# Exact attention scores in two halves of TensorE's rows, and new orders for the steps ahead of the loop

## The chip, the core and the metric

The kernel runs on one core of one Trainium2 chip. The metric is the device time of one execution in microseconds (us); smaller is better. TensorE is PE in the profile (its weight loads are PEld), VectorE is DVE, ScalarE is ACT, GpSimd is POOL, and the queue of SyncE that issues most transfers is SPq.

## The reference

64 sequences of 128 tokens and 128 features go through a block with two residual parts. Softmaxes are over keys.

```python
x = x + tanh(g_xattn) * cross_attention(layernorm(x), ctx)         # 16 heads of 8, 120 keys of ctx
x = x + tanh(g_ffn) * block(layernorm(x))
# block(x):
h = rms(x, n1_w); q = rms(heads(h @ wq.T), qn_w); k = rms(heads(h @ wk.T), kn_w); v = heads(h @ wv.T)
ao = softmax(where(causal, q @ k.T * HD**-0.5, -inf)) @ v @ wo.T   # 16 heads of 8, 128 keys
x = x + ao                                                         # features 0:32 of ao set to zero
xf = rms(x, n2_w); gates = top-2 softmax of xf @ gate_w.T          # four experts
x = x + sum_e gates_e * expert_e(xf)                               # features 0:32 of the sum set to zero
```

## The kernel before

The work is cut into 16 groups of G = 4 sequences and into five parts: N (layer norm, queries and keys of the cross attention), A (cross attention), B (queries and keys of the self attention), D (self attention and the first expert matmuls) and M (the rest of the experts). One step works on a different group in each part: M on the oldest, N on the newest. Every engine's program runs through the same list of works of a step. Four steps with lists of their own fill the pipeline (`first_group`, `second_group`, `third_group`, `fourth_group`; the text calls them the first, second, third and fourth step), twelve steps of the hardware loop share one list (`SCHEDULE`), and four more empty it (`last_queries`, `last_self_keys`, `last_self_values`, `last_experts`). A list says in which order each engine meets the works and which of the eight PSUM banks each of them takes (rings `w` of four banks, `s2` or `f` of the banks s2a and s2b, `pv`, `t`). An engine issues its instructions strictly in this order, and semaphores count how often a bank was filled and drained.

Each attention score is computed twice. The *estimate* (`s1`, L1299, bf16) gives the maximum over keys: for a sequence b and a set c of four heads, K = 32 rows of TensorE at a time; the four sets take the four row groups and four banks, and DVE reduces each bank (L1085, into `mpad`, or `mhalf` in the steps ahead of the loop). The maxima are transposed (works `mT`, or `mH` and `mL` for the first and the last two sequences apart), copied by ACT and stored by DMA as one row of the query tile `qd`. The *exact* score (`s2`, L1335, fp32r) is a matmul of 512 columns on stacks of split numbers: `kst` holds 24 rows for each of four heads and a row of ones, `qd` the four heads' queries on a block diagonal, zeros elsewhere, and the maxima in row 96, so that the maximum is subtracted on the way. ACT takes the exponential of the bank (L945, 512 columns) into a slot of `probs`; the self attention's slots are masked by POOL; then 16 small matmuls to a sequence (`pv`, L1356) multiply by the values. `exact(part, b, c)` in a list is the two sets c and c + 1 of sequence b, one in bank s2a and one in s2b: the text calls it a pair. There are 16 pairs in a step with A and D, 8 of each.

Around the exact scores the lists put estimates, values, transposes (L1218), and matmuls with all 128 rows in fp32: qk (L1267), down (L1382), the hidden layers (L1394, L1401). On `qd` and `kst` the zeros and ones are written once, before the first step; stacks are loaded by SP from `scratch`, after both operands were stored there.

## Time and profile before

| what | us |
|---|---|
| median of three runs | 1086.48 (1086.42 to 1088.23) |
| the profiled execution, its own time | 1085.92 |
| its span, from the first to the last instruction | 1084.2 |
| PE busy | 1011.1 |
| DVE busy | 790.0 |
| ACT busy | 736.9 |
| POOL busy | 338.4 |

The span holds the first step (0 to 25), the second (to 57), the third (to 98), the fourth (to 161), the twelve passes of the loop, and the four last steps. A busy TensorE is not TensorE at its peak: a matmul is counted from its issue to its last write, and matmuls overlap.

### The profile page before, as it was taken

The numbers are of one execution on the slowest core, as the hardware profiler recorded it, in microseconds if no ns is written. First come the engines' busy times: TensorE is split into PE (matmuls) and PEld (weight loads), VectorE is DVE, ScalarE is ACT, GpSimd is POOL, SyncE is SP. The second block draws the span as 40 slices with busy tenths as digits, with TensorE's granted clock in tenths as the row PEclk, the third lists the DMA queues.
The fourth block names the chain that finished last, engine by engine and source line by source line (L and its number), as shares of the span: only waits on it lengthen the run. The fifth ranks groups of instructions, "written<-read, shape, count | busy, mean of one in ns | idle before, by whom it ended". The sixth has DMA issues, their size and how long they took to land.

```text
span 1084.2 us, 26207 instructions
## 1 busy us (share of the span) xinstructions
PE 1011.1 (93%) x8649; PEld 628.9 (58%) x8649; DVE 790.0 (73%) x2172; ACT 736.9 (68%) x1334; POOL 338.4 (31%) x463
## 2 busy tenths in 40 slices
PE   7666799999999999999999999999999999999898
PEld 5343456666565566655665665566556565555465
DVE  8546787778778777877777777878777877784633
ACT  6464576677776768777676777767676777757353
POOL 5253315151330505133150514214141422404140
PEclk9779799999999999999999999999999999999999
DMA  6305233334322243333224343332233333221200
GB/s 231 121 27 195 86 101 103 127 115 143 110 94 94 90 126 124 133 114 111 93 73 124 130 127 114 123 99 84 97 129 127 114 134 104 84 67 62 68 1 19
DMA packets 77316, 114.26 MB, mean 105 GB/s; under 512 B 7776, under 2 KB 40160, under 8 KB 77152
## 3 DMA queue, kind: packets, MB, share of 16 engines
q1 hardware_dynamic: 76736, 111.51, 31.7%
q10 hardware_dynamic: 544, 2.28, 0.6%
q8 instruction: 22, 0.36, 0.1%
q14 instruction: 14, 0.11, 0.0%
HBM read 58.97 MB, written 53.74 MB: 104 GB/s over the span
## 4 chain that ended last, share of the span: by engine, by line
PE 64%; DVE 16%; ACT 13%; issue 6%; DMA 1%; ACTq 0%; POOL 0%; DVEq 0%
PE ps_pv L1356 9%; PE ps_w L1382 9%; PE ps_s2a L1335 7%; PE ps_s2b L1335 5%; PE ps_s2a L1394 5%; PE ps_s2b L1401 4%; ACT probs L945 4%; PE ps_t L1218 4%; DVE mpadB L1085 3%; PE ps_w L1401 3%; DVE mpadA L1085 3%; PE ps_w L1267 3%; PE ps_t L1369 3%; PE ps_w L1299 2%; PE ps_w L1218 2%
## 5 line engine op out<-in xcount | busy, mean ns | idle before, releaser
L945 ACT ACTIVATE probs<-ps_s2a 120x512 f32<-120x512 f32 (+1 forms) x256 | 153.6, 600 | 73.7 <-PE ps_s2a L1335 65.3
L1085 DVE TENSOR_REDUCE mpadB<-ps_w 128x4 f32<-128x512 f32 x240 | 148.8, 684 | 24.9 <-PE ps_w L1299 24.9
L1085 DVE TENSOR_REDUCE mpadA<-ps_w 128x4 f32<-128x480 f32 x224 | 131.5, 651 | 41.0 <-PE ps_w L1299 41.0
L945 ACT ACTIVATE probs<-ps_s2b 120x512 f32<-120x512 f32 (+1 forms) x256 | 153.5, 600 | 0.0
L812 POOL TENSOR_SCALAR_AFFINE_SELECT probs<-probs 128x1024 f32<-128x1024 f32 x128 | 140.2, 1095 | 0.0
L1382 PE MATMUL ps_w<-W,hid 128*128 128x96 f32 x1008 | 125.3, 278 | 1.8 <-DVE split_k L979 0.9
L1382 PEld LDWEIGHTS ps_w<-W,hid 128*128 128x128 f32 x1008 | 117.5, 192 | 12.0 <-issue 6.4
L776 POOL TENSOR_TENSOR rB<-vrB,neg_half 128x4 f32<-128x4 f32 x16 | 16.1, 1009 | 204.3 <-DVE veB L972 204.3
L1335 PE MATMUL ps_s2a<-qdA,kstA 128*120 128x512 f32 x128 | 68.5, 535 | 10.6 <-ACT probs L945 9.2
L1114 DVE SCALAR_TENSOR_TENSOR ym<-ps_w,gates,ym 128x96 f32<-128x96 f32 x192 | 47.6, 311 | 39.5 <-PE ps_w L1382 39.5
L1335 PE MATMUL ps_s2a<-qdB,kstB 128*128 128x512 f32 x128 | 65.2, 509 | 11.1 <-DMA qdB<-mTlB 4.5
L1394 PE MATMUL ps_s2a<-hid,W 128*128 128x512 f32 x152 | 74.5, 605 | 0.0
L949 ACT ACTIVATE oT<-ps_pv 128x512 f32<-128x512 f32 x64 | 38.3, 598 | 53.0 <-PE ps_pv L1356 53.0
L941 ACT ACTIVATE hid<-ps_s2a 128x512 f32<-128x512 f32 x75 | 45.0, 600 | 42.6 <-PE ps_s2a L1394 31.0
L1356 PE MATMUL ps_pv<-probs,VA 120*18 120x128 f32 x2048 | 69.3, 276 | 0.0
L1356 PE MATMUL ps_pv<-probs,VB 128*18 128x128 f32 x2048 | 69.3, 276 | 0.0
L952 ACT ACTIVATE onT<-ps_t 128x256 f32<-128x256 f32 x64 | 24.6, 385 | 61.1 <-PE ps_t L1218 61.1
L811 POOL TENSOR_TENSOR tick<-one 128x1 f32<-128x1 f32 x128 | 25.0, 196 | 127.4 <-ACT probs L945 123.6
L1356 PEld LDWEIGHTS ps_pv<-probs,VA 120*18 120x18 f32 x2048 | 50.9, 98 | 22.7 <-issue 21.4
L1356 PEld LDWEIGHTS ps_pv<-probs,VB 128*18 128x18 f32 x2048 | 50.9, 98 | 17.7 <-issue 17.1
L1335 PE MATMUL ps_s2b<-qdA,kstA 128*120 128x512 f32 x128 | 59.0, 461 | 0.0
L1369 PEld LDWEIGHTS ps_t<-W,onT 128*128 128x128 f32 x256 | 39.2, 196 | 32.4 <-issue 20.1
(276 smaller groups left out, 2133.8 us busy)
## 6 DMA issues: line engine op xcount, KB each, us to landing
scratch_Aq<-split_q SPq DMA_DIRECT2D x48, 256.0 KB, 2.4
qdA<-scratch_Aq SPq DMA_DIRECT2D x64, 192.0 KB
scratch_Bq<-split_q SPq DMA_DIRECT2D x48, 256.0 KB, 2.4
scratch_Bk<-split_k SPq DMA_DIRECT2D x48, 256.0 KB, 3.0
qdB<-scratch_Bq SPq DMA_DIRECT2D x64, 192.0 KB
kstB<-scratch_Bk SPq DMA_DIRECT2D x64, 192.0 KB
scratch_Ak<-split_k SPq DMA_DIRECT2D x48, 240.0 KB, 2.4
kstA<-scratch_Ak SPq DMA_DIRECT2D x64, 180.0 KB
```

Of the source, the lines that this page charges most:

```text
L812: pool.affine_select(out=tile, in_=tile, compare_op=ALU.is_ge, fill=0.0, base=0, pattern=[[0, 2 * HT], [1, P]], channel_multiplier=-1).the ...
L941: nc.scalar.activation(hid[:, HID_AT[index[0]] + index[1], :], bank[:], ACT.Gelu).then_inc(done, 1)
L945: nc.scalar.activation(probs[0:k, slot_of(part, *index), :], bank[0:k, :], ACT.Exp, scale=SCALE if part == "A" else 1.0).then_inc(done, 1)
L1085: nc.vector.tensor_reduce(pair[:, :, c, b % 2] if halves else mneg[p][:, :, c, b], bank[:, 0:HT * k].rearrange("p (h k) -> p h k", h=HT), ...
L1114: ins = nc.vector.scalar_tensor_tensor(out=ym[:, b, KEEP:P], in0=bank[:, b * UP:(b + 1) * UP], scalar=gates[:, b, e:e + 1], in1=y[:, b, KE ...
L1218: ins = nc.tensor.transpose(psum[st.bank[key]][:, b * P:(b + 1) * P], of(b), identf[:])
L1335: mm(o, kst[p][:, c, b * k:(b + 1) * k], qd[p][:, :, c, b * P:(b + 1) * P], start=True, stop=True).then_inc(done, 1)
L1356: ins = mm(psum[st.bank[last]][32 * j:32 * j + VS, at:at + P], VB[p][0:k, first:first + VS], probs[0:k, slot_of(part, b, c), j * P:(j + 1) ...
L1369: ins = mm(bank[:, s * n:(s + 1) * n], onT[:, s * P:(s + 1) * P], w["Wo"] if part == "A" else w["wo"], start=True, stop=True)
L1382: ins = mm(bank[:, b * UP:(b + 1) * UP], hid[:, HID_AT[h] + k, b * P:(b + 1) * P], w[f"down{index[1]}"][:, k * UP:(k + 1) * UP], start=k = ...
L1394: ins = mm(bank[:], w[name][:, k * HID + c * P:k * HID + (c + 1) * P], hid[:, HID_AT[h] + k, :], start=k == 0, stop=k == chunks[-1])
L1401: mm(bank[:], w[name][:, c * P:(c + 1) * P], xfT[:], start=True, stop=True).then_inc(done, 1)
```

## The change

An exact matmul now takes half of the rows: rows 0 to 48 hold heads 0 and 1 of a set with a row of maxima (row 48), rows 64 to 112 heads 2 and 3 with another (row 112). `qd` needs two column blocks of queries instead of four, and each half is a matmul of 49 rows and 256 columns. A pair (sets c and c + 1) becomes four such matmuls, in the order: lower half of c into bank s2a, upper half of c into s2b, lower half of c + 1 into s2a, upper half of c + 1 into s2b. So bank s2a ends with heads 0 and 1 of both sets, s2b with heads 2 and 3 of both, and the values are read from the new places. Ahead of the first of the four, PE waits for both banks to be drained; each bank's count rises with its last matmul. The number of columns, of exponentials and of DMA bytes stays. Half as many zeros are written ahead.

```diff
-        qd = {p: sb("qd" + p, [P, HT, NT, TOK], F32R) for p in "AB"}
+        qd = {p: sb("qd" + p, [P, HT // 2, NT, TOK], F32R) for p in "AB"}
...
-        M_ROW = HD * SPLIT * HT
+        HALF_ROWS, M_ROW = P // 2, HD * SPLIT * HT // 2
...
+        def rows_of_head(j):
+
+            first = j // 2 * HALF_ROWS + j % 2
+            return slice(first, first + M_ROW, 2)
...
-                        for bk, v in st.drains([], key):
-                            pe.wait_ge(drained[bk], v)
-                        o = bank[0:k, :].rearrange("p (h q) -> p h q", h=HT)
-                        mm(o, kst[p][:, c, b * k:(b + 1) * k], qd[p][:, :, c, b * P:(b + 1) * P],
-                           start=True, stop=True).then_inc(done, 1)
+                        if c % 2:
+                            continue
+                        tiles = [(part, "s2", (b, c + half)) for half in range(2)]
+                        for tile in tiles:
+                            for bk, v in st.drains([], tile):
+                                pe.wait_ge(drained[bk], v)
+                        for cc in range(2):
+                            for half in range(2):
+                                rows = slice(half * HALF_ROWS, half * HALF_ROWS + M_ROW + 1)
+                                o = psum[st.bank[tiles[half]]][0:k, cc * 2 * P:(cc + 1) * 2 * P].rearrange("p (h q) -> p h q", h=2)
+                                ins = mm(o, kst[p][rows, c + cc, b * k:(b + 1) * k], qd[p][rows, :, c + cc, b * P:(b + 1) * P],
+                                         start=True, stop=True)
+                                if cc:
+                                    ins.then_inc(filled[st.bank[tiles[half]]], 1)
...
-            clear_queries("A", 2, 3, setup_act)
...
-                            clear_queries("B", 0, HT // 2, b_cleared)
+                            clear_queries("B", 0, 1, b_cleared)
```

The lists of the second, third and fourth step are new. With them `mL` of A's first group goes by SP's queue instead of ACT's, and POOL makes the causal factor of the keys right after that of the queries, one step earlier. In `last_queries` one work moves by one place, and in `last_self_keys` the last two down matmuls take bank pv, estimate 2 stands between them, and estimate 3 stands ahead of the second half of the first expert. The loop's list is the same.

```diff
-    return (one("N", "xT", 0, "pv") + one("N", "k", 0, "t") + one("N", "q", 0, "pv") + one("A", "mL")
-            + exact("A", 0, 0) + exact("A", 0, 2) + estimate("A", 0) + exact("A", 1, 0) + exact("A", 1, 2) + values("A", 0)
+    return (one("N", "xT", 0, "pv") + one("N", "k", 0, "t") + exact("A", 0, 0) + one("A", "mL") + exact("A", 0, 2) + one("N", "q", 0, "pv")
+            + exact("A", 1, 0) + estimate("A", 0) + exact("A", 1, 2) + values("A", 0)
```

ACT's instructions at the start of the second step, before: the casts of keys and queries (L850, L855), the copy of the maxima (L915) with its transfer, then the exponentials.

```order
L850 ACTIVATE kTbA<-ps_t,vc 128x480
L855 ACTIVATE split_k<-ps_t,vc 128x480
L850 ACTIVATE qTbA<-ps_pv,vc 128x512
L855 ACTIVATE split_q<-ps_pv,vc 128x512
L915 ACTIVATE mTlA<-ps_w 32x128
L924 DMA qdA<-mTlA 1x16x128 x2
L945 ACTIVATE probs<-ps_s2a 120x512
L945 ACTIVATE probs<-ps_s2b 120x512
```

And in the changed kernel:

```order
L860 ACTIVATE kTbA<-ps_t,vc 128x480
L865 ACTIVATE split_k<-ps_t,vc 128x480
L952 ACTIVATE probs<-ps_s2a 120x512
L952 ACTIVATE probs<-ps_s2b 120x512
L922 ACTIVATE mTlA<-ps_w 32x128
L952 ACTIVATE probs<-ps_s2a 120x512
L952 ACTIVATE probs<-ps_s2b 120x512
L860 ACTIVATE qTbA<-ps_pv,vc 128x512
```

Two exponentials move ahead of the queries' casts, and the transfer leaves ACT's queue.

DVE's instructions in the third step, before: the split and the spread keys of the self attention (L979, L987), then the first maxima of its estimates (`mhalfB`), behind the output matmul's sum (L1136).

```order
L1124 RECIPROCAL rden<-ps_t 128x32
L1126 TENSOR_TENSOR on<-ps_t,rden 128x256
L1001 TENSOR_SCALAR xn<-xt,mvA,rsA 128x128 x4
L979 SCALAR_TENSOR_TENSOR split_q<-ps_w,qns,split_q 128x512
L987 TENSOR_SCALAR kdB<-kTbB,pick 128x512 x4
L979 SCALAR_TENSOR_TENSOR split_k<-ps_w,vc,split_k 128x512
L1136 SCALAR_TENSOR_TENSOR x<-ps_t,tg,xb 128x256
L1085 TENSOR_REDUCE mhalfB<-ps_s2a 128x4
L1085 TENSOR_REDUCE mhalfB<-ps_s2b 128x4
```

In the changed kernel:

```order
L986 SCALAR_TENSOR_TENSOR split_q<-ps_w,qns,split_q 128x512
L994 TENSOR_SCALAR kdB<-kTbB,pick 128x512 x4
L986 SCALAR_TENSOR_TENSOR split_k<-ps_w,vc,split_k 128x512
L1008 TENSOR_SCALAR xn<-xt,mvA,rsA 128x128 x4
L1131 RECIPROCAL rden<-ps_t 128x32
L1133 TENSOR_TENSOR on<-ps_t,rden 128x256
L1092 TENSOR_REDUCE mhalfB<-ps_w 128x4 x4
L1143 SCALAR_TENSOR_TENSOR x<-ps_t,tg,xb 128x256
L1092 TENSOR_REDUCE mhalfB<-ps_s2a 128x4
```

The split keys come ahead of the oT work (`rden`, `on`), and the first four maxima ahead of the sum.

PE's instructions from the first exact pair of the fourth step on, before: the transpose of the last maxima (L1316) stands behind the first values (L1356).

```order
L1335 MATMUL ps_s2b<-qdB,kstB 128x512
L1218 MATMUL ps_w<-identf,hb 128x128 x4
L1335 MATMUL ps_s2a<-qdB,kstB 128x512
L1335 MATMUL ps_s2b<-qdB,kstB 128x512
L1267 MATMUL ps_w<-W,hT 128x256 x4
L1335 MATMUL ps_s2a<-qdB,kstB 128x512
L1335 MATMUL ps_s2b<-qdB,kstB 128x512
L1299 MATMUL ps_w<-kdA,qTbA 128x480 x4
L1335 MATMUL ps_s2a<-qdB,kstB 128x512
L1335 MATMUL ps_s2b<-qdB,kstB 128x512
L1356 MATMUL ps_pv<-probs,VB 18x128 x16
L1316 MATMUL ps_t<-identf,mhalfB 32x128
```

In the changed kernel:

```order
L1254 MATMUL ps_w<-W,ctT 120x128 x4
L1279 MATMUL ps_w<-W,hT 128x128 x4
L1323 MATMUL ps_t<-identf,mhalfB 32x128
L1349 MATMUL ps_s2a<-qdB,kstB 128x256
L1349 MATMUL ps_s2b<-qdB,kstB 128x256
L1349 MATMUL ps_s2a<-qdB,kstB 128x256
L1349 MATMUL ps_s2b<-qdB,kstB 128x256
L1225 MATMUL ps_w<-identf,hb 128x128 x4
L1349 MATMUL ps_s2a<-qdB,kstB 128x256
L1349 MATMUL ps_s2b<-qdB,kstB 128x256
L1349 MATMUL ps_s2a<-qdB,kstB 128x256
L1349 MATMUL ps_s2b<-qdB,kstB 128x256
```

The transpose now stands ahead of the step's first pair, and each pair has four matmuls of 256 columns.

## Rows read from the trace of the kernel before

**Rows 1.** The page: busy time of each engine; the chain that ended last.

```profile
PE 1011.1 (93%) x8649; PEld 628.9 (58%) x8649; DVE 790.0 (73%) x2172; ACT 736.9 (68%) x1334; POOL 338.4 (31%) x463
PE 64%; DVE 16%; ACT 13%; issue 6%; DMA 1%; ACTq 0%; POOL 0%; DVEq 0%
```

**Rows 2.** Busy time and clock (PEclk) in four stretches.

```profile
25.00:57.00 32.00, 20.64 (x193) 11.31 (x192) 18.12 (x44) 13.98 (x27) 11.20 (x22) 0.78 0.35 112
57.00:98.00 41.00, 29.36 (x244) 18.56 (x244) 24.74 (x68) 23.47 (x43) 14.06 (x26) 0.84 0.26 87
98.00:161.00 63.00, 51.64 (x453) 31.04 (x453) 45.00 (x114) 38.74 (x74) 19.35 (x25) 0.89 0.33 108
480.00:543.00 63.00, 61.66 (x539) 38.18 (x537) 48.87 (x135) 45.85 (x86) 19.85 (x26) 1.00 0.34 113
```

**Rows 3.** Chain, same place in two passes: start, us, what.

```profile
480.09 0.23 PE ps_s2a L1335
...
542.63 0.23 PE ps_s2a L1335
```

**Rows 4.** Timeline, a pair behind an estimate and ahead of values: start, us.

```profile
489.66 0.50 PE L1335 MATMUL ps_s2a<-qdB,kstB 128*128 128x512 f32 x1
489.77 0.19 PEld L1335 LDWEIGHTS ps_s2b<-qdB,kstB 128*128 128x128 f32 x1
490.00 0.40 PE L1335 MATMUL ps_s2b<-qdB,kstB 128*128 128x512 f32 x1
490.32 0.79 PEld L1356 LDWEIGHTS ps_pv<-probs,VB 128*18 128x18 f32 x32 [0.36 <-issue]
```

**Rows 5.** Timeline, PE, a pair's second matmul ahead of transposes with 128 rows.

```profile
488.20 0.39 PE L1335 MATMUL ps_s2b<-qdB,kstB 128*128 128x512 f32 x1
488.44 0.60 PE L1218 MATMUL ps_t<-identf,oT 128*128 128x128 f32 x4
```

**Rows 6.** Timeline, weight loads of an estimate, one for each row group.

```profile
82.71 0.09 PEld L1295 LDWEIGHTS ps_s2a<-causal_k,causal_q 32*128 32x128 bf16 x1
...
82.72 0.10 PEld L1295 LDWEIGHTS ps_w<-causal_k,causal_q 32*128 32x128 bf16 x2
```

**Rows 7.** Timeline, weight loads of down, all in the same rows.

```profile
475.84 1.86 PEld L1382 LDWEIGHTS ps_w<-W,hid 128*128 128x128 f32 x16
```

**Rows 8.** Timeline, dense stretch: an exponential and weight loads of pairs.

```profile
480.88 0.60 ACT L945 ACTIVATE probs<-ps_s2b 128x512 f32<-128x512 f32 x1
...
481.54 0.19 PEld L1335 LDWEIGHTS ps_s2b<-qdB,kstB 128*128 128x128 f32 x1 [0.30 <-ACT probs L945]
...
482.97 0.19 PEld L1335 LDWEIGHTS ps_s2a<-qdB,kstB 128*128 128x128 f32 x1 [0.21 <-issue]
...
484.64 0.19 PEld L1335 LDWEIGHTS ps_s2b<-qdB,kstB 128*128 128x128 f32 x1 [0.30 <-ACT probs L945]
```

**Rows 9.** Timeline, last self values: first matmuls of two pairs in a row.

```profile
1028.25 0.48 PE L1335 MATMUL ps_s2a<-qdB,kstB 128*128 128x512 f32 x1
...
1029.42 0.49 PE L1335 MATMUL ps_s2a<-qdB,kstB 128*128 128x512 f32 x1 [0.45 <-ACT probs L945]
```

**Rows 10.** Timeline, second step: ACT's key split, first exponential, DVE behind values.

```profile
25.69 0.65 ACT L855 ACTIVATE split_k<-ps_t,vc 128x480 fp32r<-128x480 f32 x1
28.85 0.60 ACT L945 ACTIVATE probs<-ps_s2a 120x512 f32<-120x512 f32 x1 [1.23 <-issue]
47.53 1.79 DVE L1085 TENSOR_REDUCE mhalfA<-ps_w 128x4 f32<-128x480 f32 x3 [1.81 <-PE ps_w L1299]
```

**Rows 11.** Timeline, third step: transposes to queries and keys; first maximum.

```profile
76.07 1.59 PE L1218 MATMUL ps_w<-identf,qk 128*128 128x128 f32 x8
83.36 0.69 DVE L1085 TENSOR_REDUCE mhalfB<-ps_s2a 128x4 f32<-128x512 f32 x1 [1.96 <-PE ps_s2a L1299]
```

**Rows 12.** Timeline, fourth step: the wait for the last maxima.

```profile
109.08 0.29 PEld L1335 LDWEIGHTS ps_s2a<-qdB,kstB 128*128 128x128 f32 x1 [4.64 <-DMA qdB<-mTlB]
```

**Rows 13.** Timeline, last self keys: estimate 2 behind DVE's gated sums.

```profile
1011.76 0.40 PE L1295 MATMUL ps_w<-causal_k,causal_q 32*128 32x512 bf16 x4 [1.25 <-DVE ym L1114]
```

More of the change, by code:

```diff
@@ L196, in third_group @@
-            + one("A", "nT", 0, "t") + one("A", "wo", 0, "t") + values("A", 3) + one("B", "v")
-            + estimate("B", 0, "ffww") + one("N", "xT", 0, "t") + estimate("B", 1, "wwtp") + one("A", "oT", 1, "f")
-            + estimate("B", 2, "fwww") + one("A", "nT", 1, "t") + one("B", "mH", 0, "t") + estimate("B", 3, "ffwp")
+            + exact("A", 2, 0) + one("B", "sums", 0, None) + one("B", "root", 0, None) + exact("A", 2, 2)
+            + one("N", "stats", 0, None) + one("B", "init", 0, None) + values("A", 1) + one("B", "scale", 0, None)
@@ L203, in fourth_group @@
 def fourth_group():
-    order = of_parts("NABD")
-    at = order.index(("D", "s2", (2, 0), "s2"))
-    return order[:at] + one("D", "mL", 0, "t") + order[at:]
+    cross, experts = of_parts("NABD", cross_attention()), of_parts("NABD", first_experts())
+    return (one("D", "mL", 0, "t") + of_parts("NABD", self_attention())
+            + one("D", "wo", 0, "t") + estimate("A", 3) + values("D", 3) + one("D", "oT", 1, "t") + one("A", "mT")
+            + one("B", "scale", 0, None) + one("D", "nT", 1, "t") + one("D", "wo", 1, "t") + one("D", "out", 0, None)
+            + exact("A", 0, 0) + one("B", "qT") + one("B", "kT") + exact("A", 0, 2) + one("N", "stats", 0, None) + one("B", "v")
+            + one("D", "squares", 0, None) + one("N", "norm", 0, None) + one("N", "xT")
+            + cross[cross.index(("A", "s2", (1, 0), "s2")):] + experts)
@@ L664, in step @@
                         sp.dma_start(maxima_of(OP[part]), mTr[OP[part]][:].bitcast(F32)).then_inc(m_loaded[OP[part]], 16)
-                    elif work in HALVES and not maxima_by_act(st, part, work):
-                        half = HALVES.index(work)
-                        sp.wait_ge(drained[st.bank[part, work, 0]], st.fills(part, work, 0))
-                        for b in range(2):
-                            sp.dma_start(half_of_maxima(OP[part], half, b), half_source(OP[part], half, b)).then_inc(half_loaded[OP[part]][half], 16)
+                    elif work in HALVES and not maxima_by_act(st, part, work) and (st.parts, work) != ("NA", "mL"):
+                        load_half(st, part, work)
             load_x(0)
@@ L1341, in step @@
                         last = (part, "pv", (b | 1, NT - 1))
-                        sources = [(part, "s2", index)] if part == "A" else []
+                        sources = [(part, "s2", (b, c // 2 * 2 + half)) for half in range(2)] if part == "A" else []
                         if part == "D":
```

61 lines of the change are left out of this document (32 added, 29 removed).

## The prediction

> **What bounds the kernel now.** I began with the page: PE is busy for 1011 of 1084 us, and the chain that ended last runs through PE for 64%, through DVE for 16%, ACT for 13% [rows 1]. So PE binds, but not alone. The table by stretch then shows two regimes. In a pass of the loop PE is busy for 61.7 of 63 us at the full 2.4 GHz (granted clock 1.00). In the second, third and fourth step it is busy for 20.6 of 32, 29.4 of 41 and 51.6 of 63 us, with a mean clock of 0.78 to 0.89, a mix of 2.4 and 1.2 GHz [rows 2]. In the loop only less work or less waiting on PE's path counts; a pass takes 542.63 - 480.09 = 62.5 us [rows 3]. Ahead of it about 11 + 12 + 11 us of PE are idle, and there the order of the works counts.
>
> **The exact pair when nothing blocks it.** In the timeline a pair between an estimate and values starts at 489.66. The weights of its second matmul start to load at 489.77, the second matmul stands at 490.00, and the first weights of the values at 490.32 [rows 4]. So 0.11 us pass before the first matmul streams (its load is not hidden), each stream takes 0.23 (489.77 to 490.00, and as long again), and 0.09 pass from the end of the second stream at 490.23 to the next load. Ahead of work that also uses all 128 rows the second matmul is followed after 0.24 [rows 5]: no gap. I read 0.11 + 0.09 = 0.20 us as the price of a change between matmuls on 128 rows and matmuls on row or column groups. Before, a pair paid nothing at a neighbour with 128 rows (0.46 between two of them) and 0.20 across the change on both sides of the pair together with its own first load: 0.66.
>
> After, the pair is in a mode of its own, 64 rows. Do its halves run together? The nearest rows are the estimate's: weight loads for different row groups and banks start within 0.01 us [rows 6], where 16 loads into the same rows take 1.86 us, 0.116 each [rows 7]. Two halves together make a stream of 256 columns, half of 0.23; the next weights need 0.116, just as long. So the new pair streams for 2 x 0.12 = 0.23 instead of 0.46, plus 0.11 and 0.09: 0.43 in any surroundings. Bounds of one pair's stream: 0.23 (together) to 0.46 (loads one by one, 4 x 0.116); I take the first, since its nearest row is for the same array and the same kind of grouping. The price of entering or leaving lies between 0 and 0.20 for the two sides of a mode change; I take 0.20 by rows 4.
>
> The Trainium skill (TensorEngine Tiling (Array Packing), "Key Properties") says that changing the tiling mode drains TensorE, while tiles load and multiply in parallel. The trace agrees with both on 32 rows; no row shows 64. By its "Theoretical Speedup" alone, up to 2x for 64 rows, every pair would simply save half its stream.
>
> A step has 16 pairs (fourth step to the first of the last four: 14 steps with both attentions). By their neighbours in the loop's list:
> - eight stand between estimates and values: 0.66 becomes 0.43, 0.23 saved where PE isn't blocked;
> - two (first of sequence 1 in each attention) have 128-row work on one side: one more change, 0.20 - 0.23, saves 0.03;
> - six stand between 128-row works: two more changes, (0.40 - 0.23) = 0.17 lost each.
>
> **What the common wait does.** Before, the matmul into s2a started when ACT had read s2a, under the exponential of s2b. Now all four wait for both. In the dense stretch the exponential of s2b (0.60 from 480.88) ends at 481.48, and the second matmul of the next pair starts to load at 481.54 [rows 8]. The changed pair starts there as a whole and ends where the old one did: its gain is gone, and both exponentials of it, that followed at once before, come about 0.47 late (a stream and its latency). Behind a ring of two banks a pair then costs load and matmul 0.50 [rows 4], two exponentials 0.49 apart (1.09), and some 0.07 of signals: 1.66 us. Before, two pairs in a row stood 1029.42 - 1028.25 = 1.17 apart [rows 9]. What is late next: the third pair, at 482.97, would have to wait for an exponential that now ends at 481.54 + 1.62 = 483.16, 0.2 late, which its shorter stream gives back; the fourth, at 484.64 before [rows 8], can't start before 483.20 + 1.66 = 484.86. So this stretch loses about 0.2, and 0.35 with the 0.13 that its first pair brings. The same stretch of the cross attention I put at 0.1, since DVE's maxima gate the estimate in it.
>
> Sum for a pass: two outer pairs at the start of D 0.34; dense D 0.35; its last pair -0.23 (the one before it lies beside DVE's gated sums, nothing); A's first two pairs 0, they wait for ACT; dense A 0.1; A's last two 0.17 - 0.23. Together +0.5 us, times 14 = **+7 us**. The exponentials, masks, DVE's maxima and DMA bytes stay the same.
>
> **The steps ahead of the loop.** Second step: ACT has the split of the keys done at 26.34 (25.69 + 0.65), but its first exponential starts at 28.85, behind two casts of queries, the copy of the maxima and the issue of their transfer [rows 10]. The pair needs none of these; 2.5 us earlier at best. At the end three and more maxima (1.79 us from 47.53) stand on DVE ahead of the oT work that leads to hb; that order is turned around, up to 2.4. I take 4 of the 4.9. Third step: the queries' transposes stand at 76.07 behind an exact pair that waits for ACT, and the first of 16 maxima of 0.69 each (11 us) starts at 83.36, when DVE has nearly nothing else left [rows 11]. They now start between exact pairs; DVE is busy for only 24.7 of 41 us [rows 2]. Between 0 and 7 us; I take 3, since ACT then has casts and exponentials in one queue. Fourth step: PE waits 4.64 us for the last maxima's transfer [rows 12]; their transpose now stands ahead of the first pair, over 8 us earlier in the program, so the whole wait goes, and with it some of the 1.2 GHz that followed it (clock 0.89 in the stretch). The exact scores of A go ahead of the transposes to queries and keys. 4.6 + 2 = 6.6, between 4 and 9. Together 13.6, less 0.6 for pairs in a row that now take 1.66: **-13 us**. SP's queue gets one more wait (for `mL`) ahead of the keys' store, which nobody needs before the third step. The fewer zeros on ACT and POOL lie beside DVE's maxima of the first step: 0; were ACT late there, 1.9 us at most.
>
> **The last steps.** Two steps have pairs in a row without estimates: 1.66 instead of 1.17, six times, partly under values: +1.5. In the last self keys, PE waits 1.25 us for DVE's gated sums at an estimate [rows 13]; with other banks for them and that estimate between them, -2. Together about -1 with the earlier `mT`.
>
> Sum: +7 - 13 - 1 = -7. The profiled execution took 1085.9 with a span of 1084.2, 1.7 outside; the median is 1086.5. That makes 1079.5 as a median, 1079 in the profiled execution's terms. Forecast **1079**.
>
> **The rivals.**
> - *The changes are free on 64 rows* (chance 0.16). Then the six outer pairs save 0.23 instead of losing 0.17, 0.4 each, of which four lie on the path, -1.6 a pass, 14 times: -22, 1057. For it: the order of 128 and 64 rows was never seen. Against: both 32 rows and column groups pay. The Trainium skill (TensorEngine Tiling (Array Packing), "Theoretical Speedup") gives this result if its rule on draining is left aside.
> - *The common wait costs more* (0.28). One mechanism: s2a and s2b come free and full together, so ACT idles for 0.56 at each pair (fill 0.50 and signals), where before it had the other bank. It decides from the point at which more than the two dense stretches run at 1.66 a pair: 1 us more in a pass, +14, gives 1093, slower than before. Against: in a pass ACT is busy for only 45.9 of 63 us [rows 2].
> - *Weights load one half after the other* (0.11). Each pair streams 0.46 as before and pays all changes: +0.23 for every pair, 10 to 16 of them on the path: 2.3 to 3.7 a pass, 32 to 52: about 1120. Against it: rows 6.
> - *As forecast* (0.45): 1072 to 1086.
>
> **How the numbers follow.** A measurement of this kernel tells about 0.2%, 2.2 us, from no change: faster is under 1084.3, slower over 1088.7. From the cases: faster 0.45 x 0.93 + 0.16 + 0.28 x 0.25 = 0.65; slower 0.28 x 0.6 + 0.11 = 0.28; same 0.07. The range reaches from the free change, 1057, over the forecast to the costly wait, 1097, and leaves out the loads one by one and the ends beyond.
>
> **What would show it.** In the profile of after: the four matmuls of an unblocked pair within 0.35 us, pairs of starts within 0.02 (else loads in turn); from a 128-row matmul to a pair a gap of 0.1 and exposed loads (else changes are free); pass length 62.5 + 0.5; waits of PE for ACT's exponentials up from where they were, both banks at once; no wait for the last maxima in the fourth step; the loop reached about 13 us earlier. A pass over 63.6 us, or a ramp that is shorter by less than 8, makes the forecast wrong upward; a pass under 62 downward.

## The result, and the profile after

The changed kernel takes **1118.51 us** (median of four, 1113.97 to 1123.8), the kernel before 1087.36 (1086.42 to 1088.52) beside it. The ratio is 1.029, with a 95% interval of 1.024 to 1.034: slower by 31 us, where 1079 was forecast. The profiled execution took 1117.77 us with a span of 1116.0. Of all executions in this document one, of wide_added (1185.88 us), was in a slower state, and it is left out of that kernel's ratio and of its time at 1.2 GHz.

The page of after: busy time of each engine, the share of the main DMA queue (packets, MB, share of 16 engines), and the chain that ended last.

```profile
PE 993.2 (89%) x9161; PEld 636.6 (57%) x9161; DVE 791.2 (71%) x2172; ACT 735.1 (66%) x1332; POOL 336.2 (30%) x463
q1 hardware_dynamic: 76310, 111.53, 37.0%
PE 57%; ACT 17%; DVE 14%; issue 9%; DMA 1%; SPq 1%; ACTq 0%; POOL 0%; DVEq 0%
```

Against [rows 1], PE is busy for 18 us less in a run that is 32 us longer, and its share of the chain goes from 64% to 57%; ACT (13% to 17%) and "issue" (6% to 9%) gain what PE lost. The table by stretch (busy time of PE, PEld, DVE, ACT and POOL, clock, DMA share, GB/s):

```profile
25.00:57.00 32.00, 22.58 (x214) 13.15 (x211) 17.74 (x36) 14.42 (x28) 17.64 (x38) 0.68 0.42 109
57.00:98.00 41.00, 28.92 (x258) 18.56 (x259) 23.78 (x64) 21.69 (x40) 6.42 (x6) 0.71 0.36 92
98.00:161.00 63.00, 49.98 (x487) 31.22 (x486) 45.82 (x122) 40.24 (x76) 21.64 (x27) 0.84 0.40 108
300.00:900.00 600.00, 553.69 (x5302) 353.59 (x5298) 458.42 (x1256) 425.34 (x773) 184.83 (x238) 0.99 0.39 106
1050.00:1070.00 20.00, 14.45 (x121) 9.72 (x120) 4.67 (x21) 11.62 (x22) 8.40 (x14) 0.66 0.01 2
```

Two things stand out beside [rows 2]. In the loop PE is busy for 92% of the time, not 98%. And the clock has fallen: 0.68 and 0.71 ahead of the loop where it was 0.78 and 0.84, and 0.66 in a stretch of the last steps. With two levels, the time at 1.2 GHz is (1 - mean clock) x 2 x span: 41 us of the span before (clock 0.981), 121 us after (0.946).

DVE's hb (one group of four in each step) is a clean mark of the steps. The timeline of DVE, after:

```profile
226.15 1.11 DVE L1033 TENSOR_SCALAR hb<-x,mvB,rB 128x128 f32<-128x128 f32 x4
...
612.61 1.12 DVE L1033 TENSOR_SCALAR hb<-x,mvB,rB 128x128 f32<-128x128 f32 x4
...
676.18 1.11 DVE L1033 TENSOR_SCALAR hb<-x,mvB,rB 128x128 f32<-128x128 f32 x4
...
932.15 1.12 DVE L1033 TENSOR_SCALAR hb<-x,mvB,rB 128x128 f32<-128x128 f32 x4
```

and before:

```profile
223.84 1.12 DVE L1026 TENSOR_SCALAR hb<-x,mvB,rB 128x128 f32<-128x128 f32 x4
...
911.98 1.12 DVE L1026 TENSOR_SCALAR hb<-x,mvB,rB 128x128 f32<-128x128 f32 x4
```

So of the 31.8 us by which the span grew, 2.3 had come by the first mark of the loop (226.15 - 223.84), 17.9 came in eleven passes (706.0 against 688.1), and 11.6 from the last mark to the end. An undisturbed pass takes 676.18 - 612.61 = 63.57, 1.0 more than before; four of the eleven take 64.0, 65.2, 65.2 and 66.4. Set beside the forecast:

| stretch of the profiled execution | forecast | measured |
|---|---|---|
| to the first mark of the loop | -13 | +2.3 |
| eleven passes | 11 x 0.5 = +5.5 | +17.9 |
| from the last mark to the end | -1 | +11.6 |

### The profile page after: what moved, and what is told of

It is laid out like the page before. It is cut to its first block, busy times and chain, and to the rows that moved or that the text cites. A ratio compares the mean times of both kernels' runs of the same rounds, so it can differ in the third digit from the quotient of the medians.

```text
span 1116.0 us, 27503 instructions
## 1 busy us (share of the span) xinstructions
PE 993.2 (89%) x9161; PEld 636.6 (57%) x9161; DVE 791.2 (71%) x2172; ACT 735.1 (66%) x1332; POOL 336.2 (30%) x463
## 4 chain that ended last, share of the span: by engine, by line
PE 57%; ACT 17%; DVE 14%; issue 9%; DMA 1%; SPq 1%; ACTq 0%; POOL 0%; DVEq 0%
ACT probs L952 10%; PE ps_w L1399 9%; PE ps_pv L1372 9%; PE ps_s2a L1349 8%; PE ps_s2a L1411 5%; PE ps_s2b L1418 4%; PE ps_t L1225 3%; PE ps_w L1274 3%; PE ps_w L1418 3%; DVE mpadA L1092 3%; PE ps_t L1386 2%; PE ps_w L1225 2%; ACT split_q L865 2%; DVE hb L1033 1%; PE ps_w L1264 1%
## 5 line engine op out<-in xcount | busy, mean ns | idle before, releaser
L1399 PE MATMUL ps_w<-W,hid 128*128 128x96 f32 x976 | 128.0, 287 | 1.0 <-DVE split_k L986 0.9
L1399 PEld LDWEIGHTS ps_w<-W,hid 128*128 128x128 f32 x976 | 120.1, 201 | 11.3 <-issue 8.5
L1349 PE MATMUL ps_s2a<-qdA,kstA 49*120 49x256 f32 x256 | 69.4, 355 | 41.9 <-ACT probs L952 37.9
L1349 PE MATMUL ps_s2a<-qdB,kstB 49*128 49x256 f32 x256 | 65.6, 337 | 35.3 <-ACT probs L952 31.4
L1349 PEld LDWEIGHTS ps_s2a<-qdA,kstA 49*120 49x120 f32 x256 | 40.6, 200 | 93.7 <-ACT probs L952 68.0
L1349 PEld LDWEIGHTS ps_s2a<-qdB,kstB 49*128 49x128 f32 x256 | 39.3, 192 | 74.5 <-ACT probs L952 46.2
L1372 PE MATMUL ps_pv<-probs,VA 120*18 120x128 f32 x2048 | 77.3, 298 | 0.2 <-issue 0.2
L1349 PE MATMUL ps_s2b<-qdA,kstA 49*120 49x256 f32 x256 | 69.9, 356 | 0.0
L1372 PEld LDWEIGHTS ps_pv<-probs,VA 120*18 120x18 f32 x2048 | 55.3, 105 | 20.7 <-issue 12.9
L1349 PE MATMUL ps_s2b<-qdB,kstB 49*128 49x256 f32 x256 | 66.2, 340 | 0.0
```

The lines of the kernel that those rows point to most:

```text
L1349: ins = mm(o, kst[p][rows, c + cc, b * k:(b + 1) * k], qd[p][rows, :, c + cc, b * P:(b + 1) * P], start=True, stop=True)
L1372: ins = mm(psum[st.bank[last]][32 * j:32 * j + VS, at:at + P], VB[p][0:k, first:first + VS], probs[0:k, slot_of(part, b, c // 2 * 2 + j // ...
L1399: ins = mm(bank[:, b * UP:(b + 1) * UP], hid[:, HID_AT[h] + k, b * P:(b + 1) * P], w[f"down{index[1]}"][:, k * UP:(k + 1) * UP], start=k = ...
```

## Where a pass loses its microsecond

The timeline of after, PE and ACT in the dense stretch of the self attention (start, us):

```profile
489.92 0.38 PE L1349 MATMUL ps_s2a<-qdB,kstB 49*128 49x256 f32 x1
489.92 0.38 PE L1349 MATMUL ps_s2b<-qdB,kstB 49*128 49x256 f32 x1
490.14 0.28 PE L1349 MATMUL ps_s2a<-qdB,kstB 49*128 49x256 f32 x1
490.14 0.28 PE L1349 MATMUL ps_s2b<-qdB,kstB 49*128 49x256 f32 x1
490.45 0.60 ACT L952 ACTIVATE probs<-ps_s2a 128x512 f32<-128x512 f32 x1
490.94 0.59 ACT L952 ACTIVATE probs<-ps_s2b 128x512 f32<-128x512 f32 x1
491.59 0.38 PE L1349 MATMUL ps_s2a<-qdB,kstB 49*128 49x256 f32 x1 [0.66 <-ACT probs L952]
...
493.26 0.38 PE L1349 MATMUL ps_s2a<-qdB,kstB 49*128 49x256 f32 x1 [0.17 <-ACT probs L952]
...
494.94 0.38 PE L1349 MATMUL ps_s2a<-qdB,kstB 49*128 49x256 f32 x1 [0.86 <-ACT probs L952]
```

The two halves start in the same 0.01 us, and the second set 0.22 after the first: the halves do run together, as forecast. The pair at 491.59 has its values start at 492.02, 0.43 later, the forecast's figure. But the pairs stand 1.67 us apart. PE waits until both exponentials are done, and ACT then waits 0.59 for the next fill.

An undisturbed pass (from the mark at 612.61) can be laid beside one of before (from 348.92), by the starts of the same works on PE behind the transposes of hb. What each stretch loses:

| stretch of a pass | forecast | measured |
|---|---|---|
| D: first two pairs | 0.34 | 0.03 |
| D: dense stretch, first pair and the rest | 0.35 | 0.11 + 0.40 |
| D: last two pairs | -0.23 | -0.19 |
| A: first two pairs | 0 | 0.13 |
| A: dense stretch | 0.1 | 0.54 |
| A: last two pairs | -0.06 | -0.01 |

That is 1.0 together, where 0.5 was forecast. The first row shows what a change of mode costs between works with all 128 rows. The second pair of D and the qk work behind it, before:

```profile
352.53 0.47 PE L1335 MATMUL ps_s2a<-qdB,kstB 128*128 128x512 f32 x1
...
353.08 1.89 PE L1267 MATMUL ps_w<-W,hT 128*128 128x256 f32 x8
```

and after:

```profile
616.36 0.38 PE L1349 MATMUL ps_s2a<-qdB,kstB 49*128 49x256 f32 x1
...
616.79 1.99 PE L1274 MATMUL ps_w<-W,hT 128*128 128x256 f32 x8
```

From its start to the next work the pair took 0.55 before and takes 0.43 now, but it starts 1.96 behind the matmuls ahead of it (614.40) instead of 1.81 (350.72). The 0.15 that the change costs there and the 0.12 that the pair saves nearly cancel. The forecast had 0.46 for the old pair and 0.20 for the change.

In the dense stretch of A the loss is more than the pairs' spacing. Between the exponentials of A, ACT has four xf (L882) to do, and with both banks empty they stand in the chain:

```profile
522.45 0.59 ACT L952 ACTIVATE probs<-ps_s2b 120x512 f32<-120x512 f32 x1
522.92 1.27 ACT L882 ACTIVATE xf<-x,rM 128x128 f32<-128x128 f32 x4
524.09 0.59 ACT L952 ACTIVATE probs<-ps_s2a 120x512 f32<-120x512 f32 x1
524.57 0.60 ACT L952 ACTIVATE probs<-ps_s2b 120x512 f32<-120x512 f32 x1
```

The next pair can't start before 525.22, 2.13 behind the one at 523.09. In this pass, one of the four long ones, the clock then fell: the values behind the pair took 1.79 us instead of 1.07.

## The experiments

The table gives the median of each kernel, and the mean time at 1.2 GHz over its runs, from their mean clocks. All ratios are against the kernel before, run beside it.

| kernel | us | ratio (95%) | us at 1.2 GHz |
|---|---|---|---|
| before | 1087 | 1 | 46 |
| changed | 1118.5 | 1.024 to 1.034 | 122 |
| halves_only | 1136.0 | 1.040 to 1.049 | 144 |
| orders_only | 1075.7 | 0.987 to 0.990 | 38 |
| common_wait | 1119.2 | 1.027 to 1.031 | 55 |
| bank_by_bank | 1095.5 | 1.003 to 1.012 | 93 |
| rows_near | 1074.6 | 0.987 to 0.991 | 34 |
| heads_alternate | 1097.0 | 1.008 to 1.014 | 99 |
| exact_twice | 1104.3 | 1.014 to 1.021 | 79 |
| estimates_twice | 1120.3 | 1.029 to 1.033 | 102 |
| rows_64 | 1077.5 | 0.988 to 0.992 | 39 |
| wide_added | 1167.1 | 1.070 to 1.074 | 178 |
| keep_clock | 1071.3 | 0.983 to 0.986 | 15 |
| plain_added | 1076.0 | 0.986 to 0.991 | 33 |
| change_added | 1091.9 | 1.002 to 1.005 | 56 |
| halves_kept | 1091.0 | 1.001 to 1.006 | 62 |

### The two parts apart

**halves_only**: the kernel before, with the first diff of the change alone.

> The kernel before with its own lists; only the exact pairs are changed to half rows. Theory (the halves' common wait and the lower clock that follows it do the whole loss): the pass is 63.6 us as in the changed kernel, 1.0 more than before, and the mean clock falls to about 0.95; 1110 to 1122 us. Rival (the new orders do the loss, by sending the first pairs into a wait for their stacks and the steps ahead of the loop to 1.2 GHz): the clock stays at 0.97 or more, and 12 passes with 1.0 each give 1098 to 1102 us.

**orders_only**: the changed kernel, with the full-row pairs (and all the zeros) back.

```diff
...
+                        for bk, v in st.drains([], key):
+                            pe.wait_ge(drained[bk], v)
+                        o = bank[0:k, :].rearrange("p (h q) -> p h q", h=HT)
+                        mm(o, kst[p][:, c, b * k:(b + 1) * k], qd[p][:, :, c, b * P:(b + 1) * P],
+                           start=True, stop=True).then_inc(done, 1)
...
```

> The changed kernel's lists with the exact pairs of before (128 rows, 512 columns, a wait for each bank). Theory (the orders are good, and the halves spoil them): the steps ahead of the loop are shorter by 3 to 13 us, the clock stays near 0.98, the pass is 62.56; 1074 to 1084 us. Rival (the orders lose): the first exact pair waits about 3 us for its stacks, and the loop is reached no earlier than in the kernel before; 1086 to 1092 us.

1136.0 and 1075.7 us. The halves cost 49 us on the old orders and 43 on the new ones; the orders bring 11.4. halves_only took more than either theory gave; its undisturbed pass takes the 63.6 of the theory, but seven of its eleven passes between the marks are over 63.9 us. orders_only came out as its theory said. In orders_only the marks stand at 216.58 and 904.46: 7.3 us earlier into the loop, 0.3 in eleven passes, and 2.9 in the last steps. (By the mark of the fourth step it had been 7.5; 0.2 of that went again.)

### The common wait

**common_wait**: the kernel before, full-row pairs, both banks awaited ahead of the first matmul.

```diff
-                        for bk, v in st.drains([], key):
-                            pe.wait_ge(drained[bk], v)
+                        for tile in [(part, "s2", (b, c)), (part, "s2", (b, c + 1))] if c % 2 == 0 else []:
+                            for bk, v in st.drains([], tile):
+                                pe.wait_ge(drained[bk], v)
```

> The kernel before; both matmuls of a pair are unchanged, but both banks' drains are awaited ahead of the first. Theory (the common wait is the cause): pairs in the dense stretches are spaced 1.66 us or a little more, the pass grows by 1.0 to 1.8 us (a full pair streams 0.23 longer than a halved one inside the round trip), 1100 to 1115 us, and the clock falls in the steps with idle waits. Rival (changes between 128 and 64 rows are the cause): within 4 us of before.

**bank_by_bank**: the changed kernel, each bank's two half matmuls together, behind that bank's own wait.

```diff
-                        for cc in range(2):
-                            for half in range(2):
+                        for half in range(2):
+                            for bk, v in st.drains([], tiles[half]):
+                                pe.wait_ge(drained[bk], v)
+                            for cc in range(2):
```

> The changed kernel, but both halves' matmuls of one bank stand together (lower half of c, lower half of c + 1 into s2a, then the two upper halves into s2b) and each bank is awaited by itself. The streams of the halves then mostly follow one another (0.46 a pair). Theory (the common wait is the cause): the dense stretches are as short as before, and what is left is the mode change, 0.2 a pair at 10 of 16 pairs: pass 62.6 to 64, clock 0.97 or more, 1085 to 1105 us. Rival (half rows keep the clock low whatever the waits are): clock 0.95 or less, 1115 us or more.

The wait alone costs full-row pairs 32 us: 1119.2, on the old lists, where the halves with it take 1136.0. Timeline of common_wait, PE:

```profile
498.63 0.50 PE L1336 MATMUL ps_s2a<-qdB,kstB 128*128 128x512 f32 x1 [0.50 <-ACT probs L945]
...
500.31 0.50 PE L1336 MATMUL ps_s2a<-qdB,kstB 128*128 128x512 f32 x1
...
501.98 0.50 PE L1336 MATMUL ps_s2a<-qdB,kstB 128*128 128x512 f32 x1 [0.63 <-ACT probs L945]
```

They stand 1.67 apart, the same as the halves: the round trip doesn't care that a half pair streams for half as long. A pass takes 64.17. Two wrong guesses in my expectation: the spacing was not longer with full rows, and the total was 4 us over the range. One more thing stands in this run. Its clock in the loop does not fall, although PE waits there as in the changed kernel:

```profile
300.00:900.00 600.00, 562.36 (x5046) 352.04 (x5046) 455.67 (x1252) 427.58 (x777) 187.53 (x243) 1.00 0.34 109
```

All its passes between the marks take 64.16 or 64.17. So the common wait with full rows leaves the clock of the loop alone, and so do the halves without the wait (bank_by_bank, all passes 62.74 to 62.78); it fell only with both.

Without the wait, in bank_by_bank, a pass takes 62.75 at a clock of 1.00, 0.85 less than in the changed kernel and 0.2 more than before; the run is 23 us shorter than the changed kernel. The clock of the whole run, 0.958, was lower than the 0.97 that the theory wanted; the fall lies outside the loop. Its timeline, one pair with free banks and one behind ACT:

```profile
546.77 0.38 PE L1348 MATMUL ps_s2a<-qdB,kstB 49*128 49x256 f32 x1
546.78 0.38 PE L1348 MATMUL ps_s2b<-qdB,kstB 49*128 49x256 f32 x1
547.00 0.28 PE L1348 MATMUL ps_s2a<-qdB,kstB 49*128 49x256 f32 x1
547.00 0.28 PE L1348 MATMUL ps_s2b<-qdB,kstB 49*128 49x256 f32 x1
...
550.32 0.50 PE L1348 MATMUL ps_s2a<-qdB,kstB 49*128 49x256 f32 x2 [0.17 <-ACT probs L952]
...
550.81 0.50 PE L1348 MATMUL ps_s2b<-qdB,kstB 49*128 49x256 f32 x2
```

My expectation that the streams would follow one another was wrong where nothing blocks. The upper half stands third in the program, and started 0.01 us behind the first, ahead of the second in the program. That PE issues strictly in the order of its list, as said of the kernel before, does not hold between the two halves of the rows. Where ACT holds s2b, the pair splits at the bank, as before the change. So neither the alternating order nor the common wait was needed for the halves to run together.

### Late stacks

In the changed kernel the share of the DMA queue is 37.0%, in orders_only 32.2%, for the same bytes, and the pair that the new order sends ahead in the second step waits for its stacks. Timeline of after, PE:

```profile
29.34 0.57 PE L1349 MATMUL ps_s2a<-qdA,kstA 49*120 49x256 f32 x1 [3.20 <-DMA qdA<-scratch_Aq]
```

Three edits of where, or in which order, a head's 24 rows are written; the first and the third on orders_only, the second on bank_by_bank:

```diff
-                        at = slice(j, M_ROW, HT)
+                        at = slice(j // 2 * 48 + j % 2, j // 2 * 48 + 48, 2)      # rows_near
-                    for j in range(HT):
+                    for j in (0, 2, 1, 3):                                        # heads_alternate
-                        at = slice(j, M_ROW, HT)
+                        at = slice(j // 2 * 64 + j % 2, j // 2 * 64 + 48, 2)      # rows_64
```

> New orders, full-row pairs (the 1075.7 us version), and one edit: the rows of a head are loaded every second partition inside 48 partitions, as in the halves, instead of every fourth of 96. The matmuls, their clock needs and all orders stay. Theory (the narrower target makes the stack loads slower): the queue's share of the 16 engines rises from 32% to 37%, the first exact pair of the second step waits 2 to 3 us for its stacks, 1078 to 1082 us. Rival (the target's pattern is free, and the slower loads come from something else in the halves): no wait there, 1074 to 1077 us.

> The bank-by-bank version (1095.5 us), but the four stack loads of an operand are issued in the order of heads 0, 2, 1, 3, so that two loads in a row go to different halves of the partitions. Theory (loads are slow because neighbours crowd the same 48 partitions): the loads land 1 to 2 us earlier, and the time falls by 1 to 8 us with the waits and the clock behind the first pair. Rival (each load is slow by itself): no difference, 1090 to 1100 us.

> New orders, full-row pairs (1075.7 us), with the stacks placed as in the halves: heads 0 and 1 in rows 0 to 47, heads 2 and 3 in rows 64 to 111, one row of maxima at 48 (zeros between, so the result is the same); the matmuls still take 128 rows and 512 columns. Theory (the place of the upper half at partition 64 makes the stack loads slower): the queue's share of the 16 engines rises from 32% to 36% or more, the first exact pair starts 5.5 us or more behind the last load's issue instead of 4.0, and the time rises by 1 to 5 us at most. Rival (the loads are slow for another reason): share 32 to 33.5%, 1073 to 1077 us. If the clock falls for longer than before here as well, late loads alone explain the clock of the halves.

The shares of the queue in rows_near, heads_alternate and rows_64:

```profile
q1 hardware_dynamic: 76800, 111.53, 33.2%
```

```profile
q1 hardware_dynamic: 76310, 111.53, 34.9%
```

```profile
q1 hardware_dynamic: 76800, 111.53, 38.1%
```

Every second row of 48 is not what makes loads slow; the upper half's place at partition 64 is. In rows_64 the first exact pair starts 5.9 us after the last stack load left SP's queue, in rows_near 4.2, and in orders_only, where it does not wait, 4.0. Heads that alternate between the halves take it from 6.8 to 4.9, and from 37.7% to 34.9%, but nothing of the time. The late stacks are real and cheap: 1077.5 against 1075.7 us with full rows, a difference at the edge of what these runs resolve.

### The clock

Four experiments add work to TensorE and write it where other results overwrite it. **exact_twice** (on bank_by_bank): each half matmul outside the loop issued twice. **wide_added** (on bank_by_bank): outside the loop, ahead of each bank's two half matmuls, one with 128 rows and 256 columns. **estimates_twice** (on the changed kernel): each estimate's four matmuls twice. **keep_clock** (on orders_only): transposes of a constant, where PE waits for hb, qk and xn in the third and fourth step.

```diff
+                                for again in range(1 if st.parts == PARTS else 2):                  # exact_twice
...
+                            if st.parts != PARTS:                                                   # wide_added
+                                mm(psum[st.bank[tiles[half]]][0:k, 0:2 * P], kst[p][:, c + half, b * k:(b + 1) * k],
+                                   qd[p][:, :, c + half, b * P:(b + 1) * P], start=True, stop=True)
...
+                        for c in range(NT if st.parts != "N" else 0):                               # estimates_twice
+                            rows = slice(c * 32, c * 32 + 32)
+                            mm(tile[c], qTb[p][rows, b * P:(b + 1) * P], kd[p][rows, :, b * k:(b + 1) * k], start=True, stop=True)
...
+                for _ in range(n if st.parts in ("NAB", "NABD") else 0):                            # keep_clock
+                    mm(psum[st.bank[key]][:, 0:P], identf[:], identf[:], start=True, stop=True)
```

> The bank-by-bank version (1095.5 us, clock 0.958), but each exact half matmul outside the loop is issued twice into the same place (the second result overwrites the first); the loop is unchanged. Theory (the clock outside the loop is low because TensorE does less work there): the mean clock rises to 0.965 or more, and the time falls to 1082 to 1092 us. Rival (a low clock there has nothing to do with how much TensorE streams, or the added streams cost more than the clock gives): 1097 to 1110 us, 64 pairs at up to 0.23 us each.

> The bank-by-bank version (1095.5 us, clock 0.958); outside the loop each bank gets, ahead of its two half matmuls, one added matmul of 128 rows and 256 columns (its result is overwritten). The loop is unchanged. It adds as much streaming as the doubled halves did (1104.3 us, clock 0.964). Theory (the clock outside the loop falls because half the rows stand idle in the exact pairs): the mean clock rises to 0.970 or more, and the time is 1085 to 1100 us. Rival (rows do not matter to the clock): clock 0.958 to 0.965, 1100 to 1112 us.

> The changed kernel (1118.5 us, clock 0.946), but each estimate's four bf16 matmuls are issued twice, in all steps but the first; in the dense stretches TensorE waits behind them anyway. Theory (the clock falls in the loop because TensorE idles in the common waits): no pass is over 64.4 us any more, the mean clock rises to 0.96 or more, and the time is the same or lower by up to 15 us, though the four estimates outside waits cost about 0.2 us each, 13 us in all at most. Rival (the clock does not depend on it): passes of 65 and 66 us stay, and the time rises by 5 to 15 us.

> New orders, full-row pairs (1075.7 us, clock 0.983), and added fp32 matmuls of 128 columns (16, 16, 8 and 16) where TensorE waits 4.4 us for hb, 2.2 us for hb, 2.5 us for qk and 5.3 us for xn in the third and fourth step; they write to the bank that the awaited transposes overwrite. Theory (the low clock behind these waits costs time, some 27 us at half clock in all): the clock rises to 0.987 or more, and the time falls by 2 to 8 us to 1068 to 1074. Rival (there TensorE is not the bound, or the added work is in the way): 1075 to 1080 us.

exact_twice: slower by 9 us, 79 us at 1.2 GHz instead of 93. The clock, 0.964, just missed the 0.965 of the theory, and the time lies in the rival's range: the added streams cost more than the clock gave. wide_added refuted its theory in full, and its rival too: 1167.1 us, with 178 us at 1.2 GHz, nearly twice as much as without the added work. Its timeline of PE shows what it adds besides streams:

```profile
38.95 0.57 PE L1346 MATMUL ps_s2a<-qdA,kstA 128*120 128x256 f32 x1
39.45 0.78 PE L1351 MATMUL ps_s2a<-qdA,kstA 49*120 49x256 f32 x2
40.16 0.57 PE L1346 MATMUL ps_s2b<-qdA,kstA 128*120 128x256 f32 x1
40.65 0.78 PE L1351 MATMUL ps_s2b<-qdA,kstA 49*120 49x256 f32 x2
```

Ahead of the weights of each of these four rows PEld stands idle for 0.22 to 0.41 us, and each of the four loads starts together with its matmul: none is hidden behind the stream before it. A pair takes 2.4 us (38.95 to the values at 41.36), where bank_by_bank takes 0.7 at this clock with free banks. The two added streams account for some 0.5 of the difference (an estimate: 512 columns take 0.23 at 2.4 GHz [rows 4], so 256 take as long at 1.2); the rest, some 1.2, stands at the four changes.

estimates_twice: all eleven passes take 64.04 to 64.06 us and the loop stays at 1.00. The passes of 65 and 66 us are gone, so the falls of the clock in the loop do depend on what PE does around its waits. The added matmuls cost 0.45 a pass, the mean clock rose to 0.954 and not to the 0.96 of the theory, and in sum nothing was won. keep_clock came out as its theory said: 1071.3 us, 4.4 less than orders_only, with 15 us at 1.2 GHz instead of 38. By stretch:

```profile
25.00:57.00 32.00, 25.80 (x240) 16.20 (x241) 19.77 (x47) 16.89 (x33) 20.50 (x40) 0.95 0.34 115
57.00:98.00 41.00, 33.95 (x330) 22.96 (x332) 27.62 (x73) 26.17 (x51) 9.53 (x11) 0.96 0.39 127
98.00:161.00 63.00, 56.38 (x555) 36.01 (x547) 48.88 (x129) 43.22 (x81) 22.43 (x29) 0.97 0.39 125
```

wide_added put the change of mode under suspicion. The next two add the same matmul of 128 columns ahead of each full-row pair outside the loop, once on 49 rows, once on 128; **halves_kept** is bank_by_bank with keep_clock's transposes.

```diff
+                        if st.parts != PARTS and c % 2 == 0:      # change_added; plain_added has [:, c, ...] and [:, 0, ...]
+                            mm(bank[0:k, 0:P], kst[p][0:49, c, b * k:(b + 1) * k], qd[p][0:49, 0, c, b * P:(b + 1) * P],
+                               start=True, stop=True)
```

> New orders, full-row pairs (1075.7 us, clock 0.983, 36 us at half clock); outside the loop one matmul of 49 rows and 128 columns is added ahead of each pair, into a place that the pair overwrites, so that the pair has a change of mode in front of it, and one more if its neighbour takes 128 rows. All streams of the pairs stay. Theory (the changes of mode themselves lead to the low clock): the time at half clock rises to 60 us or more, and the run is slower than the control with the same matmul on 128 rows by 5 us or more. Rival (the clock falls only where the pair's own streams are shorter or on half the rows): clock within 0.003 of the control, and the difference is what the gaps themselves take, 0.1 to 0.2 us at 64 pairs, most of it beside ACT: under 5 us.

> Control of the run before: the same kernel with the same matmul of 128 columns ahead of each pair outside the loop, but on all 128 rows, so without a change of mode. Expected under both theories: 0.06 to 0.12 us for each of 64 pairs, most of it beside ACT: 1074 to 1080 us, clock 0.98 or more.

> The bank-by-bank version of the halves (1095.5 us, 92 us at half clock) with the added transposes of the version that took 1071.3 us, where TensorE waits for hb, qk and xn in the third and fourth step. Theory (idle waits between the works start the low clock there, in the halves too): the clock of the third and fourth step rises as it did with full rows, the time falls by 4 us or more for the 4.4 us of there, to 1083 to 1091 us. Rival (with halves the clock stays low by the pairs themselves): time at half clock falls by less than 15 us, 1091 to 1100 us.

A half-row matmul ahead of each of 64 pairs costs 15.9 us more than the same matmul on all rows (1091.9 against 1076.0), 0.25 a pair. That is the price of one or two changes of mode with the clock behind them, not of the gap alone. Time at 1.2 GHz is 48 to 66 us in eight runs against 24 to 43 in four: more, but under the 60 that I had asked for in the mean (56). The last self values show it at one place. In plain_added, PE:

```profile
1023.89 0.44 PE L1344 MATMUL ps_s2a<-qdB,kstB 128*128 128x512 f32 x1
1024.22 0.50 PE L1344 MATMUL ps_s2b<-qdB,kstB 128*128 128x512 f32 x1
```

and the same pair in change_added, with the half-row matmul in front:

```profile
1032.51 0.47 PE L1341 MATMUL ps_s2a<-qdB,kstB 49*128 49x128 f32 x1 [0.26 <-ACT probs L951]
1032.90 0.79 PE L1344 MATMUL ps_s2a<-qdB,kstB 128*128 128x512 f32 x1
1033.50 0.63 PE L1344 MATMUL ps_s2b<-qdB,kstB 128*128 128x512 f32 x1
```

In these two executions the same pair stands at 2.4 GHz without the changes of mode and at 1.2 GHz with them; its first matmul takes 0.60 to the second instead of 0.33. halves_kept, at 1091.0 on the edge of both its ranges, gains 4.5 us over bank_by_bank, as much as the transposes gave with full rows (4.4), and 31 us at half clock, where the rival had less than 15. So with the waits filled the halves still cost 19.7 us (1091.0 against 1071.3), as without (19.8): filling these waits does not touch what the halves cost.

## Why the prediction was wrong

- **What failed, in short**: outside the loop the forecast gave the halves 0.6 us ahead of it and 1.5 behind it, and they cost 9.6 and 14.5; it gave the orders ahead of the loop 13.6, and they brought 7.3; in the loop it put the common wait of the dense A stretch at 0.1, which measured 0.54, and the falls of the clock at nothing, which measured 6.4 in eleven passes.
- **The pair itself**: 0.43 us with its halves together was right, and free changes and loads one by one are out. The terms that were built on it for a pair between works with 128 rows were not: 0.34 forecast for the first two pairs of D, 0.03 measured, since the pair before took 0.55 there and not 0.46, and the change 0.15 and not 0.20. This error went in the kernel's favour and hid part of the others. The Trainium skill (TensorEngine Tiling (Array Packing), "Key Properties") says that changing the tiling mode drains TensorE. These runs agree (the changed pair starts 0.15 us later behind the same matmuls).
- **The common wait, in the dense D stretch**, was right in mechanism: 1.66 forecast for a pair and 1.67 measured. The stretch lost 0.51 where 0.35 was forecast. **In the dense A stretch** the term was mis-sized: 0.1 forecast, 0.54 measured. I read there that DVE's maxima gate the estimate, and did not follow ACT's queue, where xf now stands between two exponentials that nothing overlaps. So a pass loses 1.0 instead of 0.5, 14 us instead of 7. That is half of what the rival "the common wait costs more" put there (1 us more in a pass, 1093); its price was not met in the pass, and 1118.5 lies far beyond it.
- **The term that was missing** is the clock. Rows 2 showed me 0.78 to 0.89 ahead of the loop, and I counted on it only as a gain ("some of the 1.2 GHz that followed it" would go). I asked of every added wait what it costs in time and never what TensorE's clock does behind it. It fell in four of eleven passes (6.4 us over 63.6 in all), and outside the loop, where each pair is a mode of its own between waits. In the loop it took the common wait and the shorter pairs together: common_wait and bank_by_bank, which have one of the two each, have no long pass, and neither has estimates_twice, which has both and more matmuls around the waits. Outside it, waits and changes of mode both take part: keep_clock and halves_kept show the first (23 and 31 us less at 1.2 GHz), change_added the second (56 against 33).
- **The steps ahead of the loop**: forecast -13, with the halves' 0.6 in it. The orders alone give -7.3 for the 13.6 forecast. The second step gave 3.8 of the 4; the third 1.1 of 3; the fourth 2.6 of 6.6. The wait for the last maxima [rows 12] did go, but in the new order xT stands behind N's norm, and PE waits there instead. Timeline of orders_only, PE:

```profile
125.24 1.11 PE L1224 MATMUL ps_w<-identf,xn 128*128 128x128 f32 x4 [5.27 <-DVE xn L1007]
```

  I took the stall as gone and did not ask what is late next. With the halves on top, 9.6 of the gain were lost again by the first mark of the loop, so that it was reached 2.3 us later instead of 13 earlier.
- **The last steps**: the orders gave -2.9 where -2 was forecast; the halves cost 14.5 from the last mark on, where I had put 1.5 for six pairs in a row. There pairs stand between waits of 1.2 to 1.5 us, at a clock of 0.66 in one stretch.
- **In sum**, against orders_only the halves cost 42.8 us: 23.0 by the common wait (changed against bank_by_bank), 19.8 by the halves without it. The marks of the profiled executions say where:

| against orders_only | to the first mark | eleven passes | behind the last mark |
|---|---|---|---|
| bank_by_bank | +12.6 | +2.4 | +5.2 |
| changed | +9.6 | +18.1 | +14.5 |

  So the common wait did its harm in the loop and in the last steps; ahead of the loop the halves cost as much without it. (Executions of bank_by_bank lie up to 12 us apart, so the 3 us there say nothing. With full rows and the old lists the wait does cost there: the first mark stands at 234.47 in common_wait and at 223.84 before.) Of the 19.8 some 2 are the late stacks and 2.6 the twelve passes; the rest, about 15, lies outside the loop in gaps at changes of mode and the clock. change_added prices such changes at 15.9 there, but it is a neighbouring edit, not the same, and how the 15 split between the gaps and the clock stays open.

The best kernel is neither of the two: the new orders with full-row pairs take 1075.7 us, and with the filled waits 1071.3 (ratio 0.983 to 0.986).

## What to carry to other kernels

A matmul that is split to save streaming must keep the waits of the whole one: if two banks come free one after the other, a pair that waits for both turns two overlapping round trips into one long one, here 1.67 us whatever the pair streams. Before a matmul moves to fewer rows, count the places where its neighbours use another tiling: in the full loop each cost little here, outside it 0.25 us with the clock. When an edit lengthens idle time on TensorE, price the clock behind it from the profile's own rows at 1.2 GHz; and where an engine waits for a known time, harmless matmuls into a bank that is about to be overwritten can be worth trying (4.4 us here, more than the new order of any one step brought).

## What the runs showed of the hardware

- Half-row matmuls for the other row half overtake one that is earlier in the program when their bank is free: third in order, started 0.01 us behind the first (bank_by_bank at 546.77).
- With the common wait, the clock fell in four (changed) and in seven (halves_only) of eleven passes of the loop where the pairs take half rows, and in none where they take all rows (common_wait, 1.00 from 300 to 900 us).
- Stacks that are written to partitions 0 to 47 and 64 to 111 load more slowly than the same rows in 0 to 95: 38.1% against 33.2% of the 16 engines for the same bytes, and the first pair starts 5.9 against 4.2 us behind the last issue (rows_64 and rows_near).
- Adding matmuls can lower the clock: 178 us at 1.2 GHz with added full-row matmuls between half-row ones, 93 without.
